# Routing in two halves through buckets in DRAM, woven into the attention and the expert tiles

## The reference, cut to what matters

```
x: (16, 256, 256), context: (16, 120, 256); all float32, 4096 tokens of 256 numbers
x = x + cross_attention(layernorm(x), context)        # 16 heads of 16
x = x + ffn(layernorm(x))                             # shared part and 8 experts
x = x + masked_cross_attention(layernorm(x), context, mask)   # one head of 256
x = x + quantised_linear(layernorm(x))

ffn(flat):                                            # flat: (4096, 256)
  probs = softmax(flat @ gate_W)                      # (4096, 8)
  topk_w, topk_idx = top_k(probs, 2)                  # ties: the lower index
  topk_w = topk_w / topk_w.sum()
  out = 0.5 * gelu(flat @ shared_W + shared_b)
  for e in 8 experts:
      h = gelu(flat @ W1[e] + b1[e])                  # 1024 wide
      out += combine[:, e] * (h @ W2[e] + b2[e])      # combine: topk_w, else 0
  out = layernorm(out) * gamma + beta
```

## Time and profile before

| | us |
|---|---|
| median of three runs | 1074.01 |
| profiled execution | 1070.92 |
| its span, first to last instruction | 1069.1 |
| busy: PE / DVE / ACT / POOL | 945.4 / 560.1 / 497.1 / 539.3 |

### The profile page before, as it was taken

How to read it: one execution, slowest core, us unless ns; L and a number is a source line. 1 busy time by engine, 2 the same in 40 slices (tenths; PEclk the granted TensorE clock), 3 DMA queues, 4 the chain that set the end, 5 groups by cost and what they waited for, 6 DMA issues and landing times.

```text
span 1069.1 us, 21031 instructions
## 1 busy us (share of the span) xinstructions
PE 945.4 (88%) x7159; PEld 808.6 (76%) x7159; DVE 560.1 (52%) x1231; ACT 497.1 (46%) x1257; POOL 539.3 (50%) x654
## 2 busy tenths in 40 slices
PE   6999999999823699999999999999999989787776
PEld 4777777777612699999999999999999978554544
DVE  3888888888769223433223223322322313679882
ACT  3666666666642233333333333333333324666663
POOL 2333333333325455555565565555556532578883
PEclk9999999999955799999999999999999998999998
DMA  5434343433217521222221221222222244122201
GB/s 142 142 111 152 100 153 101 156 103 135 80 22 203 148 41 30 41 37 35 41 40 31 41 40 32 40 40 33 39 41 36 35 91 118 43 76 90 90 33 35
DMA packets 74709, 80.11 MB, mean 75 GB/s; under 512 B 12752, under 2 KB 69904, under 8 KB 74480
## 3 DMA queue, kind: packets, MB, share of 16 engines
q1 hardware_dynamic: 58704, 60.12, 18.6%
q0 software_dynamic: 15904, 18.66, 11.1%
HBM read 52.51 MB, written 26.25 MB: 74 GB/s over the span
## 4 chain that ended last, share of the span: by engine, by line
PE 60%; DVE 20%; issue 8%; POOL 6%; ACT 5%; DMA 2%; POOLq 0%; SPq 0%; DVEq 0%; ACTq 0%
PE b_H L1269 24%; PE b_Y L1281 23%; DVE a_max L635 5%; DVE a_probs L641 4%; PE a_T L506 2%; ACT a_probs L738 2%; PE a_S L496 2%; PE b_xT L1256 1%; PE c_g_ps L1940 1%; PE c_v_ps L1945 1%; POOL a_rstd L401 1%; PE c_f_ps L1911 1%; DVE a_xin L625 1%; ACT c_xn L1804 1%; DVE c_x L1773 1%
## 5 line engine op out<-in xcount | busy, mean ns | idle before, releaser
L1435 ACT ACTIVATE b_hiddenT<-b_H,b_b 128x128 f32<-128x128 f32 x568 | 162.4, 368 | 331.9 <-PE b_H L1269 331.9
L1269 PEld LDWEIGHTS b_H<-b_rowsT,b_w 128*128 128x128 f32 x2272 | 266.6, 193 | 6.0 <-ACT b_rowsT L1444 2.4
L1269 PE MATMUL b_H<-b_rowsT,b_w 128*128 128x128 f32 x2272 | 267.3, 276 | 1.8 <-ACT b_rowsT L1444 1.8
L1281 PE MATMUL b_Y<-w_sb,b_hiddenT 128*128 x1136 | 256.8, 379 | 0.0
L1227 POOL DMA_INDIRECT ffn_rows<-b_y,scatter_idx x71 | 154.0, 2169 | 193.7 <-DVE b_y L1360 185.2
L1281 PEld LDWEIGHTS b_Y<-w_sb,b_hiddenT 128*128 128x128 f32 x1136 | 210.5, 190 | 25.7
L1356 DVE TENSOR_TENSOR b_y<-b_Y,b_bc 128x256 f32<-128x256 f32 x71 | 30.2, 425 | 324.1 <-PE b_Y L1281 324.1
L1349 DVE COPY b_w<-w_sb 128x2048 f32 x71 | 87.1, 1227 | 37.5 <-issue 26.0
L635 DVE TENSOR_REDUCE a_max<-a_S 128x8 f32<-128x960 f32 x64 | 73.6, 1149 | 26.9 <-PE a_S L496 25.1
L1213 POOL DMA_INDIRECT b_rows<-xn_rows,gather_idx x71 | 73.5, 1035 | 21.5 <-issue 19.7
L744 ACT COPY a_probsT<-a_T 120x512 f32<-120x512 f32 x128 | 69.1, 594 | 28.1 <-PE a_T L506 28.1
(11 more groups left out here) (219 smaller groups left out, 1367.2 us busy)
## 6 DMA issues: line engine op xcount, KB each, us to landing
w_sb<-in_L_ffn_W SPq DMA_DIRECT2D x32, 512.0 KB, 4.5
a_xin<-in_x SPq DMA_DIRECT2D x16, 256.0 KB, 3.0
a_xres<-in_x SPq DMA_DIRECT2D x32, 128.0 KB, 2.0
xn_rows<-a_xn SPq DMA_DIRECT2D x32, 128.0 KB, 2.3
x_rows<-a_x SPq DMA_DIRECT2D x32, 128.0 KB, 2.0
ffn_rows<-shared SPq DMA_DIRECT2D x2, 2048.0 KB, 18.6
c_x<-x_rows SPq DMA_DIRECT2D x16, 256.0 KB, 2.7
c_acc<-ffn_rows SPq DMA_DIRECT2D x16, 256.0 KB, 2.7
```

What stands on the lines that cost most here:

```text
L1269: j = pe.matmul(H_ps[i][:, c * P:(c + 1) * P], w1c[i][:, k * HID + c * P:k * HID + (c + 1) * P], xT[:, k * P:(k + 1) * P], start=(k == 0), ...
L1281: j = pe.matmul(y_ps[i][:, 0:D], hT[i][:, c * P:(c + 1) * P], w2_sb[:, bass.ds(e * (HB * D) + c * D, D)], start=(c == 0), stop=(c == HB - 1))
L1435: j = act.activation(hT[i][:, c * P:(c + 1) * P], H_ps[i][:, c * P:(c + 1) * P], ACT.Gelu, bias=b1c[i][:, c:c + 1])
```

## The change

The routing phase goes. Its work is split in two halves of 16 tiles (`GT`), and its pieces stand in the lists of the other phases.

* Tables are replaced by buckets in DRAM: 4096 entries of 8 bytes (token number, weight) for each expert. `fill_buckets` fills them with a spare row number. `count` on PE gives each choice its rank within its expert, `places` the entry, and `put` writes 128 entries by one indirect DMA from POOL: 64 puts, 32 for each half.
* The first half is chosen in DVE's attention tiles 18 to 20 (`choose`, eight parts), counted in tile 21, tabled in tiles 22 to 25 (`table`, four parts), and put by POOL in tiles 22 to 29, four puts a tile. `constants`, 19 POOL instructions, stand in POOL's tile 1. In POOL's tile 31 stands `prefetch`: four reads of bucket entries (`slots`) and three gathers.
* 24 expert tiles (`EARLY_TILES`) are formed from whole tiles that the first half fills. The second half is chosen, counted and tabled beside expert tiles 0 to 9 and put beside tiles 7 to 19, two or three puts a tile; the other 47 tiles need it.
* `slots` replaces the gather of weights; the rows are gathered, and the results scattered, by the token number in what `slots` read.
* The shared product is stored tile by tile (`store_shared`, 32 of 128 KB) into `shared_rows`. In expert tiles 0 to 3 SP loads it in chunks of 512 KB into two buffers, ACT takes the gelu of two chunks a tile (128x1024 each), and SP stores each to `ffn_rows`: `store_chunk(c)` waits for the gelu of chunk c, `load_chunk(c + 2)` for store c to have landed. The first scatter waits for all eight stores, so results are kept in seven `y` buffers instead of two, and in tiles 5 to 8 POOL issues two scatters a tile.
* `b1`, `b2` are loaded in the attention. The preparations move from tiles 4 to 10 to tiles 8 to 14. The mask's load and `bounds` move into the second phase: SP loads the mask behind the 8 contexts and ahead of the rows x, and DVE runs the eight instructions ahead of everything else of that phase. There `EARLY` is 7, and cycles -1 to 7 project one context each. ACT's wait for `c_tie`, a constant that POOL sets behind its last scatter, moves from the head of the phase to its first use.

```diff
@@ routing @@
+    def put(pool, t, k):
+        g = t // GT
+        pool.wait_ge(s_place, g + 1)
+        pool.wait_ge(s_w, 2 * g + 2)
+        pool.wait_ge(s_fill, 64)
+        pool.indirect_dma_start(bucket_d, IndirectOffsetOnAxis(place[:, t, k:k + 1], 0),
+                                pay[:, t, k, :], None).then_inc(s_put[g], 16)
...
+    def count(pe, g, at):
...
+        pe.matmul(at, before_b[:], flat, start=True, stop=False, skip_group_check=True)
+        pe.matmul(at, ones_b[:], base_b[g][:].rearrange("p t e -> p (t e)"), start=False, stop=False,
+                  skip_group_check=True)
+        for n in range(1, GT + 1):
+            i = pe.matmul(at[:, n * E:RANKS], ones_b[:], flat[:, 0:RANKS - n * E], start=False,
+                          stop=(n == GT), skip_group_check=True)
@@ attention, POOL @@
+                if t == 1:
+                    routing.constants(pool)
+                for n in puts_in(t):
+                    routing.put(pool, n // 2, n % 2)
+                if t == TILES - 1:
+                    prefetch(pool)
             add_beta(TILES - 2)
             residual(TILES - 1)
@@ attention, DVE, at the end of tile t @@
+                if routing.GT + 2 <= t <= routing.GT + 4:
+                    for part in range(3):
+                        if 3 * (t - routing.GT - 2) + part < 8:
...
+                            routing.choose(dve, 0, 3 * (t - routing.GT - 2) + part)
+                if t == COUNTED:
+                    routing.places(dve, 0)
+                if COUNTED < t <= COUNTED + 4:
+                    routing.table(dve, 0, t - COUNTED - 1)
@@ experts, SP @@
+            load_chunk(0)
+            load_chunk(1)
+            for c in range(CHUNKS):
+                store_chunk(c)
+                if c + 2 < CHUNKS:
+                    load_chunk(c + 2)
@@ experts, POOL @@
-            def body(n, i, first, last):
+            for n in range(NS):
                 if n + AHEAD - 1 < NS:
-                    gather(n + AHEAD - 1)
-                if n + 2 < NS:
-                    gather_weight(n + 2)
-                if not first:
-                    scatter(n - 1, 1 - i)
-                if last:
-                    scatter(n, i)
+                    gather(pool, n + AHEAD - 1)
+                for j in puts_at(n):
+                    routing.put(pool, routing.GT + j // 2, j % 2)
+                if n + AHEAD < NS:
+                    slots(pool, n + AHEAD)
+                for j in scatters_at(n):
+                    if j == added:
+                        scatter(j)
+                        added += 1
@@ experts, ACT, behind gelu(n + 1) and keep_rowsT(n + 2) @@
+                if n < CHUNKS // PER_TILE:
+                    for c in range(PER_TILE * n, PER_TILE * (n + 1)):
+                        gelu_chunk(c)
@@ second phase @@
-        EARLY = 8
+        EARLY = 7
-            return range(EARLY + 2 * (c + 1), EARLY + 2 * (c + 2)) if -1 <= c <= 2 else ()
+            return range(EARLY + c + 1, EARLY + c + 2) if -1 <= c < B - EARLY - 1 else ()
...
+            for part in range(B // 4):
+                bounds(part)
...
+                act.wait_ge(s_tie, 1)
...
-            act.wait_ge(s_tie, 1)
```

852 lines of the change are left out of this document (447 added, 405 removed).

## The result

The changed kernel takes 1090.77 us (median of 4 runs, 1089.73 to 1092.29), the one before 1073.28 (4 runs, 1071.09 to 1078.31): ratio 1.0159, 95% interval 1.0133 to 1.0186. 1055 was forecast, with a range to 1075. It is outside.

What follows compares the result with a forecast made beforehand. Bound by PE beside the expert tiles, by DVE alone in routing, with hardly any DVE slack in attention; -46.7 + 20 (attention) + 20 (expert tiles) - 10.5 (second phase) = -17, forecast 1055 us, range 1030 to 1075.

Steps and rivals of the forecast that it cites:

- Logits to the second tile: From last logits to the second expert tile's first product, 61.2 us shrink to 14.4: -46.7 us.
- DVE in the attention: Routing pieces added to DVE at the ends of attention tiles 18 to 25: +10 us, could be 5 or 13.
- POOL's puts in the attention: Four puts a tile on POOL delay the residual, showing after even tiles only: +4 us, from 0 to 12.
- Four are 5.0 us a tile ... 0.8 shows: Attention puts at 1.25 us each make the residual 2.1 us late, of which 0.8 reaches DVE's statistics.
- The end: Prefetch ahead of residual 31 at the attention's end delays the first expert tile: +5 us.
- Chunks: Expert tiles: loading and storing 512 KB chunks, two in 11 us, makes ACT late: +8 us, from 0 to 26.
- POOL beside the tiles: Expert tiles: POOL's 24 us of arrears, partly covered by gathers three tiles ahead: +10.5 us, from 0 to 45.
- Second phase: Without the early c_tie wait and with one context a cycle, the second phase gains: -10.5 us, from -14 to 0.
- The sum itself: Whole kernel: -46.7 + 20 + 20 - 10.5 = -17 on the profiled 1070.9 gives 1054; forecast 1055 us.
- The rival with POOL as the bound: Puts wait under DVE's weight copies or cost as much as a scatter, 1.7 us: slower, 1083; chance 0.13.
- Its other half: Puts begun under DVE's weight copies wait up to 1.23 us, 0.1 on average, some +3 us.
- The signs I had named: Expert tiles beginning near 326, ACT waiting 3 to 4 us for chunks, PE waiting for rows in tiles 10 to 20.

Runs made afterwards that it cites:

- e2: Changed kernel with the first half's 32 puts in the attention left out, so it computes something else: 1077.0 us.
- e4: Changed kernel with the four puts of each attention tile spread among POOL's other work instead of four in a row: 1080.6 us.
- e12: e11 with the shared product in 16 chunks of 256 KB and four buffers, and the prefetch behind tile 31's residual and inverse deviations: 1066.6 us.
- e6: e4 without chunks: the shared product's gelu left out, the attention storing straight into the ffn rows, no scatter waiting for chunks: 1060.5 us.
- e5: e4 without the second half's 32 puts beside the expert tiles, so it computes something else: 1050.0 us.
- e1: Kernel before with two second-phase edits only: seven contexts projected ahead, then one a cycle, and ACT's c_tie wait moved to first rounding: 1063.8 us, ratio 0.9916.
- e14: Changed kernel with each of the attention's 32 puts replaced by an indirect write of 1 KB a row, four in a row: 1103.8 us.
- e7: e4 with the second half chosen earlier, 12 of its puts in expert tiles 3 to 5, then two a tile, and POOL reordered: 1073.7 us.
- e13: e12 without POOL's waits for landed puts, places ready earlier, 16 puts in tiles 1 to 4, a memset behind each second one: 1072.4 us.
- e9: Changed kernel where each attention put waits until the one before it has landed: 1138.1 us.
- e15: e12 with a POOL memset behind every indirect DMA of expert tiles 3 to 5 instead of waits for landed puts: 1065.3 us, ratio 0.9930.
- e11: e7 with pairs of puts in expert tiles 3 to 5 waiting for earlier ones to land, then one a tile, later two: 1070.6 us.

## Why the forecast was wrong

* *Logits to the second tile* (-46.7): right, -46.1. The pieces were 3.3, 6.5, 1.5 and 3.8 us, where 3.3, 5.8, 1.5 and 3.8 had been worked out.
* *DVE in the attention* (+10): right, 12.1 (6.8 before tile 22; 83.6 - 78.3 = 5.3 behind it in e2, without puts, where 2.9 was forecast).
* *POOL's puts in the attention* (+4): **wrong, 24.3.** The step that failed is "Four are 5.0 us a tile ... 0.8 shows". The length was right (0.96 and 0.30). What was missing is an effect on an engine that has nothing to do with the put: PE's signals arrive up to 4.3 us late under indirect writes back to back, and DVE and ACT stand still meanwhile. No row of before could show it, because it never issues two indirect writes without a wait between. The bound from both sides, 0 and 12, was drawn from the put's duration alone, and it was too narrow. Spread, the puts cost 2.1 (e4).
* *The end* (+5): right, 4.7, and e12 takes 4.1 of it away.
* *Chunks* (+8): 9.7, with a round of 5.7 us for the 5.5 worked out. By the Trainium skill (DMA: Bandwidth & Descriptors, Anatomy of one DMA) it would have been near +4, an estimate; the section is about DMAs issued by GpSimd, these are issued by SP, and the earlier trace rows decided against it, rightly. Not in the sum: the chunks hold the first scatter until 403.7, and without them e6 is 13 us better than their own part explains.
* *POOL beside the tiles* (+10.5): **too small, 28.5** (e5), inside my bounds of 0 to 45. Two steps failed. A round with one scatter was taken as 8.2 us and is 9.0, and three with two scatters, 33.8 together by the sum, took 36.2: arrears of 33.8 us from 413.53 on, where 22 were reckoned. And the gathers' lead of three tiles was to cover 13 of them; POOL enters this stretch late by the chunks, and of 33.8 us of arrears 29.5 show.
* *Second phase* (-10.5): -9.5 in the changed kernel's profile, of which 4.8 come from the first normalisation (18.0 us behind the last b_Y; 15.4 in e1). It waits there for the rows of `ffn_rows`, which land 11.9 us behind the last b_Y:

```profile
919.18 0.75 DVE L1797 BATCH_NORM_STATS2 c_acc_bn<-c_acc 128x6 f32<-128x256 f32 x2 [5.84 <-DMA c_acc<-ffn_rows]
```

That this term came out so well is in part luck: with the same program of the phase the other profiles give -1.4 to -7.0, all but e6 at a lower clock in its first 43 us (0.78 to 0.88 for 0.92). The sum itself has a slip too: -17 from a median of 1074.0 is 1057, and why it became 1055 isn't said. It makes no difference to the outcome.

The rival with POOL as the bound (slower, 1083, 0.13) came closest in time, but not by its mechanism: a put takes 0.96 us in the median, not 1.7. Its other half, puts that wait while DVE copies weights, is real and small (8 of the 32 late ones, 0.7 us each). The signs I had named did speak: POOL's arrears show as PE waiting for rows in tiles 9 to 21, ACT waits 3.5 to 4.7 us for chunks, and the last logits are there at 345.8 instead of 326.

## What to carry to other kernels

Price what you add to an otherwise idle queue also by what it does to the others: 32 indirect writes, four in a row on POOL, cost PE's consumers 24 us; the same 32 among POOL's other work cost 2. Two edits that share an engine need a common budget: chunks and late puts each fitted beside the tiles, and the scatter that waits for the one starts the arrears of the other. Time the small independent part by itself: here it gained 9.0 us alone, and nothing else in the change added to that. And ask, before a cause is put down to an edit, whether the run it is compared with shows the effect at all: here a whole group of traces showed none.

## What the runs showed of the hardware

* Indirect writes to DRAM issued 1.27 us apart by POOL, four in a row, went with signals of PE that arrive up to 4.3 us late (rows of 8 bytes, the changed kernel) and 3.6 us late (rows of 1 KB, e14). With gathers among them it was 3.6 us in e7 and 15.5 us in e13. Seven reads in a row: 0.5 us. Spread among POOL's other work: 1.0 us at most. The signals of DVE, ACT and POOL that are on record are not late.
* The delay is not in every trace. e1 to e4, e9 to e12 and e15 have none, also where they issue the same DMAs in the same order. By what path it happens, what decides between the two kinds, whether an operation of POOL between two writes stops it or only the spacing, and whether a plain write on another queue does the same is open.
* An indirect DMA that overlaps DVE's float32 copy of weights takes 0.5 to 0.8 us longer (0.97 to 1.68 for a put, 0.99 to 1.44 and 1.78 for a gather, 1.61 to 2.11 for a scatter).
* Loads and stores of 512 KB went from 5.7 to between 6 and 9 us a round with puts beside them. This was seen in e7 and e11, and e13's chunks of 256 KB waited up to 4.2 us for their load; which of the two, the writes or POOL's descriptors, slows them was not separated.
